# A four-layer graph network on one core: node stages load and store two groups of rows at a time

## The chip, the cores and the metric

The kernel runs on one core of one Trainium2 chip. The metric is device time in microseconds for one execution. Times before: 3703.67 us median of 3 runs, 3701.21 to 3707.44.

## What is computed

A table x of 50000 nodes by 128 numbers (fp32) and 25000 edges (src, dst, type), sorted by dst, go through four layers. Each layer normalises the rows of x, takes the positive part, applies a graph layer, and adds the result to x:

```python
h = jnp.maximum(_layernorm(x, axis=-1), 0.0)
x = x + _L0_gnn_ref(h, ...)   # per relation: sum over edges of h[src] @ w[type], + h @ loop + bias, relu
x = x + _L1_gnn_ref(h, ...)   # attention over edges, 4 heads, summed by src
x = x + _L2_gnn_ref(h, ...)   # two mean-aggregating layers, each with a layernorm
x = x + _L3_gnn_ref(h, ...)   # degree-normalised sum of h[src] @ W, and a self loop
```

## The kernel before, in words

There are five phases: REL (layer 0), ATT (layer 1), SAGE0 and SAGE1 (layer 2), GCN (layer 3). Each has an edge stage and then a node stage. The edge stage gathers rows by src with indirect transfers from POOL, multiplies them, sums them by destination within tiles of 128 edges, and scatters the sums to the table sums (attsums in ATT). In SAGE0, SAGE1 and GCN the sums of the edge stage are parked in SBUF and scattered in 49 rounds while the node stage already runs; load_s is then held until the rounds that it needs have landed (a value load of the due round, L648, and a wait).

**Node stage.** The 50000 rows are cut into 98 groups of 512 rows; in a group each partition holds K = 4 consecutive rows. A row has W = 132 numbers, 128 data and 4 columns for scales, 528 bytes; a group is 264 KB in 128 pieces of 2112 bytes. (In REL the input x, and in GCN the output, have 128 columns: 256 KB.) A ring of 16 slots, one group each, holds 8 slots for x, 4 for the sums and 4 for the output; in SAGE1 it is 4, 4 and 8.

All five engines run their own list of stages with lags (run_steps, L80 to 97): in turn t a stage with lag n works on group t-n. An engine does its list strictly in order, so a wait in one stage holds all that follow. The lists that matter:

- SP (L613 to 685) issues every transfer of the node stage: load_x, lag 0; load_s, lag 2 (ATT 0, SAGE1 3); load_x2, SAGE1 only, lag 5; store, lag 9 (ATT 6, SAGE1 10, GCN 7). In REL also row_stored (L675), lag 11, which tells POOL that rows are in memory. In REL load_s(g) waits until PE's products(g-4) are done, in GCN too, in SAGE0 for add_mean(g-4), in SAGE1 for mid_sd(g-4) on ACT, in ATT for weigh_heads(g-4). store(g) waits for row_ready(g).
- PE (L1286): products (L1321, L1324), lag 3, then the transposes turn_rows (L1299), lag 1, in REL and GCN; lags 2 and 0 in SAGE0 and SAGE1. The products go to 4 PSUM banks in turn in REL and SAGE1, 2 in SAGE0 and GCN.
- ACT in REL: roots of variances (L1044, L1095), take_turned (L1070), then normalise (L1056, n_h), lag 1.
- DVE in REL, in this order: statistics of x, lag 0; in_scales (L1715), lag 1; add_product (L1751), lag 4, which writes the output slot; out_scales (L1736); in_shifts (L1730), lag 1, after which ACT may normalise; out_shifts (L1743), lag 6, which gives row_ready; the statistics of the output, lag 5.
- DVE in ATT: denominators, out_scales (lag 3), inverses, statistics of the output (lag 2), out_shifts (L1743, lag 3, row_ready), weigh_heads (L1774, lag 0). POOL does add_x (L879), which writes the output slot. In GCN DVE's last stage, finish_gcn (L1836, lag 4), writes the output slot and gives row_ready. In SAGE0 mid_rows (L1799, lag 6) does so; add_mean (L1785) has lag 3.

What writes an output slot first waits in out_free (L516), until the store of the group that had the slot (four back, eight in SAGE1) has landed. The signals for transfers are semaphores of 8 slots each: loaded, loaded_s, loaded2, stored.

After REL's node stage POOL fetches destination rows for ATT (L855), in rounds held back by row_stored. Each phase begins when the stores of the one before have landed.

Of the kernel before, what the change touches and what calls it, by code (L numbers as in the profile page):

```python
# [5 lines left out]
class Step:  # L6
# [97 lines left out]
def gnn_stack_kernel(nc, x, src, dst, edge_type, w_rel, w_loop, b_loop, w_q, w_k, w_v,  # L104
# [9 lines left out]
    N, D = x.shape  # L114
# [25 lines left out]
    GROUPS = -(-N // GROUP)  # L140

    SLOTS = 8
    RING = 16
# [17 lines left out]
    with ctx:  # L161
# [213 lines left out]

        loaded = [Signal(sem(f"loaded{s}"), 16) for s in range(SLOTS)]
        loaded_s = [Signal(sem(f"loaded_s{s}"), 16) for s in range(SLOTS)]
        loaded2 = [Signal(sem(f"loaded2_{s}"), 16) for s in range(SLOTS)]
        stored = [Signal(sem(f"stored{s}"), 16) for s in range(SLOTS)]
# [78 lines left out]
        def stores_before(phase, s):  # L458

            return phase * (GROUPS // SLOTS + (1 if s < GROUPS % SLOTS else 0))  # L460

# [20 lines left out]
        def dense(slot):  # L482

            return ring_cells[:, slot * K * W:slot * K * W + K * D].rearrange("p (k d) -> p k d", k=K)
# [5 lines left out]
        def x_cols(phase, g, c):  # L490

            if phase == REL:
                at = g.mod(8) * K * W + K * D + (c - COL_A) * K
                return ring_cells[:, at:at + K]
            return x_rows(phase, g)[:, :, c]

        def x_col(phase, g, k, c):

            if phase == REL:
                at = g.mod(8) * K * W + K * D + (c - COL_A) * K + k  # L500
# [7 lines left out]
        def x_landed(eng, phase, g):  # L508
            s = g.mod(SLOTS)
            eng.wait_ge(loaded[s].sem, loaded[s].after(g.div(SLOTS), stores_before(phase, s)))  # L510

        def s_landed(eng, phase, g):
            s = g.mod(SLOTS)
            eng.wait_ge(loaded_s[s].sem, loaded_s[s].after(g.div(SLOTS), stores_before(phase, s)))

        def out_free(eng, phase, g):  # L516
# [36 lines left out]
        def _(sp):  # L553
# [35 lines left out]
            for phase in range(5):  # L589
# [11 lines left out]
                if phase > 0:  # L601
                    for s in range(SLOTS):
                        sp.wait_ge(stored[s].sem, 16 * stores_before(phase, s))

                def span(g):
                    if g.i is None and g.offset == GROUPS - 1:
                        return slice(N - GROUP, N)
                    return bass.ds(g.scaled(GROUP), GROUP)
# [4 lines left out]
                def load_x(g):  # L613
                    s = g.mod(SLOTS)
                    if phase == REL:

                        sp.wait_ge(n_y_used.sem, n_y_used.before(g, SLOTS, first(MATMUL, phase)))
                    elif phase == ATT:

                        sp.wait_ge(x_added.sem, x_added.before(g, SLOTS))  # L620
                    elif phase == SAGE0:

                        sp.wait_ge(n_turned.sem, n_turned.before(g, SLOTS, first(MATMUL, phase)))
                    elif phase == SAGE1:

                        sp.wait_ge(n_turned.sem, n_turned.before(g, 4, first(MATMUL, phase)))
                    else:

                        sp.wait_ge(row_ready.sem, row_ready.before(g, SLOTS, phase * GROUPS))
                    table = node_in[phase]  # L630
                    sp.dma_start(x_data(phase, g) if phase == REL else x_rows(phase, g), table[span(g), :].rearrange("(p k) c -> p k c", k=K))\
                        .then_inc(loaded[s].sem, 16)

                def load_s(g):
                    s = g.mod(SLOTS)
                    if phase == ATT:
                        sp.wait_ge(weighted_ready.sem, weighted_ready.before(g, S_SLOTS))
                    elif phase == SAGE0:
                        sp.wait_ge(n_y_used.sem, n_y_used.before(g, S_SLOTS, first(MATMUL, phase)))
                    elif phase == SAGE1:  # L640
                        sp.wait_ge(mid_sd_ready.sem, mid_sd_ready.before(g, S_SLOTS, first(MID_NORM, phase)))
                    else:
                        sp.wait_ge(n_y_ready.sem, n_y_ready.before(g, S_SLOTS, first(MATMUL, phase)))
# [1240 lines left out]
```

## Time and profile before

| | |
|---|---|
| median of 3 runs | 3703.67 us (3701.21 to 3707.44) |
| profiled execution | 3701.02 us, span 3699.3 us |
| busy in the span | PE 71%, PE weight load 62%, DVE 68%, ACT 53%, POOL 71% |
| granted TensorE clock | 0.895 of full speed |
| REL node stage | about 612 to 990 us |
| ATT node stage | about 1657 to 1920 us |
| SAGE0 node stage | about 2190 to 2502 us |
| SAGE1 node stage | about 2770 to 3125 us |
| GCN node stage | about 3400 to 3699 us |
| SP's and ACT's transfers | 241758 packets, 502.00 MB, 41.0% of 16 DMA engines |
| POOL's transfers | 90944 packets, 133.85 MB, 16.3% |

Busy time is that of instructions that compute; issuing a transfer is not counted. A stretch's DMA share is the mean busy share of 16 DMA engines. The idle time named before an instruction is put down to what came last by the profile.

### The profile page before, as it was taken

How to read it: one execution, taken by the hardware profiler on the slowest of the kernel's cores; microseconds unless marked ns; L12 is line 12 of the kernel's file. 1: busy time of each engine (PE TensorE's matmuls, PEld its weight loads, DVE VectorE, ACT ScalarE, POOL GpSimd, SP SyncE). 2: the span in 40 equal slices, each digit the busy share in tenths (PEclk: the TensorE clock that was granted, in tenths of full speed). 3: DMA queues.
4: the chain of work that ended last, by engine and by line, in shares of the span. 5: the costliest groups of instructions: out<-in, count | busy, mean ns of one | idle time of the engine just before them, and what ended most of it. 6: DMA issues, size and time to landing. Idle time of an engine off the chain costs nothing. (4 is left out here: it accounts for less than half of the span.)

```text
span 3699.3 us, 82926 instructions
## 1 busy us (share of the span) xinstructions
PE 2617.9 (71%) x19724; PEld 2288.0 (62%) x19724; DVE 2511.4 (68%) x11513; ACT 1948.6 (53%) x5393; POOL 2612.2 (71%) x2673
## 2 busy tenths in 40 slices
PE   3899998888466666630018887767888775887888
PEld 3899997666465555530007765546776665776777
DVE  5677776889555445538864448883448887665998
ACT  1333334777454444421117777763446664776777
POOL 3677773666788888855457778767778784777876
PEclk9999999999787777765559999998999998999999
DMA  7544444888433333339972239982229997222998
GB/s 277 215 149 140 147 147 136 268 267 269 125 42 41 41 41 41 41 50 317 311 229 53 52 109 297 294 287 67 52 60 332 335 337 246 53 52 79 309 311 287
DMA packets 336597, 638.73 MB, mean 173 GB/s; under 512 B 62000, under 2 KB 90832, under 8 KB 335208
## 3 DMA queue, kind: packets, MB, share of 16 engines
q1 hardware_dynamic: 241758, 502.00, 41.0%
q0 software_dynamic: 90944, 133.85, 16.3%
q10 hardware_dynamic: 3786, 1.65, 0.2%
q8 instruction: 41, 0.67, 0.1%
q14 instruction: 68, 0.56, 0.0%
HBM read 371.35 MB, written 277.50 MB: 175 GB/s over the span
## 5 line engine op out<-in xcount | busy, mean ns | idle before, releaser
L750 POOL DMA_INDIRECT got<-rows,gidx x588 | 606.3, 1031 | 225.8 <-issue 173.3
L797 POOL DMA_INDIRECT sums<-got,sidx x588 | 614.9, 1046 | 168.7 <-issue 156.5
L1056 ACT ACTIVATE n_h<-ring 128x128 f32<-128x128 f32 x1176 | 482.7, 482 | 56.5 <-DVE ring L1730 45.8
L971 ACT ACTIVATE psum_out<-bank 128x132 f32<-128x132 f32 x784 | 218.8, 279 | 531.4 <-PE bank L1223 530.7
L1324 PE MATMUL bank<-ring,ident 128*128 128x128 f32 x2352 | 459.3, 277 | 0.0
L1204 PE MATMUL bank<-parked 128*128 128x128 f32 x3136 | 388.7, 278 | 11.9 <-DVE parked L1558 11.9
L1189 PE MATMUL bank<-ident,e_h 128*128 128x128 f32 x588 | 96.0, 287 | 408.0 <-ACT e_h L934 408.0
L1204 PEld LDWEIGHTS bank<-parked 128*128 128x128 f32 x3136 | 371.5, 194 | 13.7 <-issue 8.6
L811 POOL DMA_INDIRECT attsums<-ring,sidx x196 | 312.3, 1594 | 80.2 <-issue 64.5
L1324 PEld LDWEIGHTS bank<-ring,ident 128*128 128x128 f32 x2352 | 361.6, 194 | 0.0
L1461 DVE COPY gidx<-src_i 128x4 int32 (+1 forms) x227 | 45.2, 199 | 465.2 <-DMA got<-rows,gidx 204.4
L1223 PE MATMUL bank<-psum_out,eq 128*128 128x132 f32 x1568 | 351.7, 306 | 12.2 <-ACT psum_out L971 9.7
L1219 PE MATMUL bank<-msg,eq 128*128 128x132 f32 x1568 | 322.5, 287 | 24.5 <-issue 17.8
L1299 PE MATMUL bank<-ident,n_h 128*128 128x128 f32 x1176 | 200.1, 295 | 194.3 <-ACT n_h L1056 191.1
L1321 PE MATMUL bank<-w_t,n_ht 128*128 128x128 f32 x1568 | 284.6, 296 | 64.0 <-DMA ring<-sums 63.7
L1189 PEld LDWEIGHTS bank<-ident,e_h 128*128 128x128 f32 x588 | 65.5, 143 | 427.5 <-ACT e_h L934 409.7
L934 ACT ACTIVATE e_h<-got 128x128 f32<-128x128 f32 x588 | 282.5, 484 | 41.7 <-DMA got<-rows,gidx 34.2
L855 POOL DMA_INDIRECT got<-rows,didx x196 | 197.0, 1005 | 143.4 <-SPq L678 76.6
L1321 PEld LDWEIGHTS bank<-w_t,n_ht 128*128 128x128 f32 x1568 | 221.9, 198 | 117.0 <-DMA ring<-sums 90.9
L1299 PEld LDWEIGHTS bank<-ident,n_h 128*128 128x128 f32 x1176 | 129.2, 145 | 248.4 <-ACT n_h L1056 248.1
L1223 PEld LDWEIGHTS bank<-psum_out,eq 128*128 128x128 f32 x1568 | 236.1, 190 | 67.5 <-ACT psum_out L971 25.3
L1558 DVE SCALAR_TENSOR_TENSOR parked<-bank,e_ht 128x256 f32<-128x256 f32 x784 | 267.9, 417 | 9.4 <-PE bank L1159 7.8
(183 smaller groups left out, 7250.7 us busy)
## 6 DMA issues: line engine op xcount, KB each, us to landing
ring<-sums SPq DMA_DIRECT2D x392, 264.0 KB
ring<-rows SPq DMA_DIRECT2D x392, 264.0 KB, 4.7
rows<-ring SPq DMA_DIRECT2D x294, 264.0 KB
attsums<-parked SPq DMA_DIRECT2D x49, 528.0 KB
rows<-parked SPq DMA_DIRECT2D x49, 528.0 KB
ring<-attsums SPq DMA_DIRECT2D x98, 264.0 KB
rowsg<-ring SPq DMA_DIRECT2D x98, 264.0 KB
ring<-rowsg SPq DMA_DIRECT2D x98, 264.0 KB
```

Of the source, the lines that this page charges most:

```text
L750: pool.indirect_dma_start(out=got[:, b, j, 0:width], out_offset=None, in_=table[:, :], in_offset=bass.IndirectOffsetOnAxis(ap=gidx[:, b, j ...
L797: pool.indirect_dma_start(out=sums[:, :], out_offset=bass.IndirectOffsetOnAxis(ap=sidx[:, b, j:j + 1], axis=0), in_=got[:, b, j, :], in_of ...
L811: pool.indirect_dma_start(out=attsums[:, :], out_offset=bass.IndirectOffsetOnAxis(ap=sidx[:, b, j:j + 1], axis=0), in_=att_out[:, b, j, :] ...
L934: last = nc.scalar.activation(e_h[:, b, j, :], got[:, c, j, 0:D], ACT.Relu, bias=got[:, c, j, COL_C:COL_C + 1], scale=got[:, c, j, COL_A:C ...
L1056: last = nc.scalar.activation(n_h[:, b, k, :], x_data(phase, g)[:, k, :], ACT.Relu, bias=x_col(phase, g, k, COL_C), scale=x_col(phase, g, ...
L1204: last = nc.tensor.matmul(o, lhsT=e_htm[:, h, rel, at:at + P], rhs=w_rel_sb[:, rel, :], start=(rel == 0), stop=(rel == NREL - 1))
L1219: nc.tensor.matmul(o, lhsT=eq[:, b, j, 0, :], rhs=msg[:, b, j, :], start=True, stop=False)
L1223: nc.tensor.matmul(o, lhsT=eq[:, b, j, 1, :], rhs=carried, start=False, stop=True)\
L1299: last = nc.tensor.transpose(bank[b][:, k * P:(k + 1) * P], rows, ident[:, :])
L1321: last = nc.tensor.matmul(o, lhsT=n_ht[:, b, k * P:(k + 1) * P], rhs=node_w[phase], start=(bias is None), stop=(not summed and k == K - 1))
L1324: last = nc.tensor.matmul(o, lhsT=ident[:, :], rhs=s_rows(phase, g)[:, k, 0:D], start=False, stop=(bias is None or k == K - 1))
L1558: last = nc.vector.scalar_tensor_tensor(out=e_htm[:, h, rel, :], in0=type_bank[b][:, at:at + 2 * P], scalar=float(rel), in1=e_ht[:, b, at: ...
```

## The change

Groups are loaded and stored by pairs. A pair is 1024 rows, and each partition holds eight consecutive rows of it: four in the even group's slot, four in the odd one's. Every transfer of a node stage moves 528 KB in 128 pieces of 4224 bytes (512 KB in 4096 where a row has 128 columns). An odd group's load and an even group's store do nothing; a load waits for what its later group (g+1) needs, a store for the odd group's row. The number of slots, the lags and the work by group on the engines stay. The semaphores count by pair, four of each kind. The last pair is the last 1024 rows, which overlap the pair before. row_stored adds 2 for each pair.

```diff
+    def pair(self):
+        return self.back(self.offset % 2).div(2)
...
+    PAIR = 2 * GROUP
+    PAIRS = GROUPS // 2
...
+    PSLOTS = SLOTS // 2
...
         def out_free(eng, phase, g):
             back = OUT_SLOTS.get(phase, 4)
             if g.i is None and g.offset < back:
                 return
-            o = g.back(back)
-            s = o.mod(SLOTS)
-            eng.wait_ge(stored[s].sem, stored[s].after(o.div(SLOTS), stores_before(phase, s)))
+            o = g.back(back).pair()
+            s = o.mod(PSLOTS)
+            eng.wait_ge(stored[s].sem, stored[s].after(o.div(PSLOTS), stores_before(phase, s)))
...
                 def load_x(g):
-                    s = g.mod(SLOTS)
+                    if g.offset % 2:
+                        return
+                    s = g.pair().mod(PSLOTS)
+                    later = g.back(-1)
                     if phase == REL:
-                        sp.wait_ge(n_y_used.sem, n_y_used.before(g, SLOTS, first(MATMUL, phase)))
+                        sp.wait_ge(n_y_used.sem, n_y_used.before(later, SLOTS, first(MATMUL, phase)))
...
                     table = node_in[phase]
-                    sp.dma_start(x_data(phase, g) if phase == REL else x_rows(phase, g), table[span(g), :].rearrange("(p k) c -> p k c", k=K))\
+                    sp.dma_start(slot_pair(g.mod(X_SLOTS.get(phase, 8)), table.shape[1]), rows_of(table, g))\
                         .then_inc(loaded[s].sem, 16)
...
                 def load_s(g):
-                    s = g.mod(SLOTS)
+                    if g.offset % 2:
+                        return
+                    s = g.pair().mod(PSLOTS)
+                    later = g.back(-1)
...
-                        sp.wait_ge(n_y_ready.sem, n_y_ready.before(g, S_SLOTS, first(MATMUL, phase)))
+                        sp.wait_ge(n_y_ready.sem, n_y_ready.before(later, S_SLOTS, first(MATMUL, phase)))
...
-                        due = sp.value_load(due_i[0:1, CHASED.index(phase), at(g)], min_val=base, max_val=base + ROUNDS)
+                        due = sp.value_load(due_i[0:1, CHASED.index(phase), at(later)], min_val=base, max_val=base + ROUNDS)
...
                 def store(g):
-                    s = g.mod(SLOTS)
+                    if g.offset % 2 == 0:
+                        return
+                    s = g.pair().mod(PSLOTS)
                     sp.wait_ge(row_ready.sem, row_ready.after(g, phase * GROUPS))
...
                     table = node_out[phase]
-                    sp.dma_start(table[span(g), :].rearrange("(p k) c -> p k c", k=K),
-                                 out_data(phase, g) if phase == GCN else out_rows(phase, g)).then_inc(stored[s].sem, 16)
+                    slots = OUT_SLOTS.get(phase, 4)
+                    sp.dma_start(rows_of(table, g), slot_pair(RING - slots + g.back(1).mod(slots), table.shape[1]))\
+                        .then_inc(stored[s].sem, 16)
```

slot_pair gives two neighbouring slots as one run of cells in each partition, rows_of the table's 1024 rows as eight to a partition. Where rows have 128 columns, the data of the two groups now stand side by side in the pair of slots, with the scale columns behind them (dense, dense_col).

## Rows read from the trace of the kernel before

**Rows 1.** Stretches REL to GCN: us, busy PE, PEld, DVE, ACT, POOL, PEclk, DMA, GB/s

```profile
627.00:961.00 334.00, 287.94 (x2034) 232.21 (x2031) 298.84 (x1990) 249.18 (x665) 213.26 (x267) 0.99 0.86 260
1662.00:1914.00 252.00, 0.00 (x0) 0.00 (x0) 222.36 (x1254) 28.55 (x96) 124.95 (x98) 0.50 0.93 308
2217.00:2497.00 280.00, 196.49 (x1167) 141.48 (x1166) 230.91 (x1019) 209.32 (x537) 212.33 (x256) 0.94 0.91 293
2777.00:3119.00 342.00, 270.37 (x2007) 226.59 (x2007) 306.18 (x1253) 212.23 (x680) 254.76 (x275) 0.98 0.97 329
3414.00:3697.00 283.00, 239.37 (x1938) 218.82 (x1937) 255.63 (x1421) 221.83 (x570) 210.21 (x270) 1.00 0.94 301
```

**Rows 2.** Waits in REL's node stage: us in total, times, longest

```profile
DVE ring L1751 <- DMA rows<-ring: 27.7, 40, 1.5
...
SPq L650 <- PE bank L1324: 171.6, 93, 9.6
```

**Rows 3.** Timeline of REL's node stage: start us, us, engine, line, operation

```profile
796.25 0.38 SPq L671 DMA_DIRECT2D rows<-ring  x1
...
796.50 0.17 DVE L1743 SCALAR_TENSOR_TENSOR ring<-out_mv,ring 128x4 f32<-128x4 f32 x1
...
799.71 0.35 SPq L671 DMA_DIRECT2D rows<-ring  x1
799.78 0.69 DVE L1751 SCALAR_TENSOR_TENSOR ring<-bank,ring 128x512 f32<-128x512 f32 x1 [0.71 <-DMA rows<-ring]
...
800.48 0.13 DVE L1730 SCALAR_TENSOR_TENSOR ring<-in_mv,ring 128x4 f32<-128x4 f32 x1
...
800.69 1.65 ACT L1056 ACTIVATE n_h<-ring 128x128 f32<-128x128 f32 x4 [0.67 <-DVE ring L1730]
...
802.78 0.16 DVE L1715 RECIPROCAL ring<-in_sd 128x4 f32<-128x4 f32 x1
...
803.81 0.69 DVE L1751 SCALAR_TENSOR_TENSOR ring<-bank,ring 128x512 f32<-128x512 f32 x1 [0.87 <-DMA rows<-ring]
...
804.97 0.39 PE L1324 MATMUL bank<-ring,ident 128*128 128x128 f32 x2
...
806.11 0.35 SPq L671 DMA_DIRECT2D rows<-ring  x1
```

**Rows 4.** Waits in ATT's node stage

```profile
POOL ring L879 <- DMA rows<-ring: 96.1, 64, 2.3
```

**Rows 5.** Timeline of ATT's node stage

```profile
1675.32 0.34 SPq L671 DMA_DIRECT2D rows<-ring  x1
...
1678.46 1.26 POOL L879 TENSOR_TENSOR ring<-n_t,ring 128x512 f32<-128x512 f32 x1 [1.10 <-DMA rows<-ring]
...
1785.95 1.26 POOL L879 TENSOR_TENSOR ring<-n_t,ring 128x512 f32<-128x512 f32 x1 [2.14 <-DMA rows<-ring]
1786.08 1.15 DVE L1743 SCALAR_TENSOR_TENSOR ring<-out_mv,ring 128x4 f32<-128x4 f32 x1
```

**Rows 6.** Timeline of SAGE1's node stage

```profile
2903.17 0.31 ACT L1078 ACTIVATE mid_sd<-mid_mv,eps_col 128x4 f32<-128x4 f32 x1
...
2904.68 0.33 SPq L650 DMA_DIRECT2D ring<-sums  x1
...
2909.17 0.49 PE L1321 MATMUL bank<-w_t,n_ht 128*128 128x128 f32 x2 [0.38 <-DMA ring<-sums]
```

**Rows 7.** Timeline of GCN's node stage

```profile
3523.65 1.13 DVE L1836 SCALAR_TENSOR_TENSOR ring<-bank,ring 128x128 f32<-128x128 f32 x4
...
3530.23 0.35 SPq L671 DMA_DIRECT2D out_dram<-ring  x1
```

**Rows 8.** SP's DMA queue, 150 to 550 us and 1700 to 1900 us: packets, MB, share

```profile
q1 hardware_dynamic: 10656, 40.01, 26.5%
...
q1 hardware_dynamic: 33228, 62.40, 95.1%
```

**Rows 9.** A stretch of ATT's edge stage, columns as in rows 1

```profile
1200.00:1250.00 50.00, 28.73 (x183) 26.38 (x183) 25.68 (x105) 22.41 (x66) 40.84 (x31) 0.77 0.33 40
```

More of the change, by code:

```diff
@@ L374, in gnn_stack_kernel @@
                     a_h, a_turned, a_ht, a_qkv, a_q, a_logit, a_exp, a_res, a_sum, a_out, a_eq]
[L376 to L379, printed above, removed]
+        loaded = [Signal(sem(f"loaded{s}"), 16) for s in range(PSLOTS)]
+        loaded_s = [Signal(sem(f"loaded_s{s}"), 16) for s in range(PSLOTS)]
+        loaded2 = [Signal(sem(f"loaded2_{s}"), 16) for s in range(PSLOTS)]
+        stored = [Signal(sem(f"stored{s}"), 16) for s in range(PSLOTS)]
         in_var = Signal(sem("in_var"), 1)
@@ L492, in x_cols @@
             if phase == REL:
[L493 removed]
+                at = dense_col(g.mod(8), c)
                 return ring_cells[:, at:at + K]
@@ L508, in x_landed @@
         def x_landed(eng, phase, g):
[L509 to L510 removed]
+            p = g.pair()
+            s = p.mod(PSLOTS)
+            eng.wait_ge(loaded[s].sem, loaded[s].after(p.div(PSLOTS), stores_before(phase, s)))
         def s_landed(eng, phase, g):
[L513 to L514 removed]
+            p = g.pair()
+            s = p.mod(PSLOTS)
+            eng.wait_ge(loaded_s[s].sem, loaded_s[s].after(p.div(PSLOTS), stores_before(phase, s)))
         def out_free(eng, phase, g):
@@ L601, in _, with rows_of @@
                 if phase > 0:
-                    for s in range(SLOTS):
+                    for s in range(PSLOTS):
                         sp.wait_ge(stored[s].sem, 16 * stores_before(phase, s))
[L605 to L608, printed above, removed]
+                def rows_of(table, g):
+                    p = g.pair()
+                    if p.i is None and p.offset == PAIRS - 1:
+                        at = slice(N - PAIR, N)
+                    else:
+                        at = bass.ds(p.scaled(PAIR), PAIR)
+                    return table[at, :].rearrange("(p k) c -> p (k c)", k=2 * K)
                 def at(g):
@@ L677, in row_stored @@
-                    sp.wait_ge(stored[s].sem, stored[s].after(g.div(SLOTS), stores_before(phase, s)))
-                    sp.sem_inc(rows_stored.sem, 1)
+                    if g.offset % 2 == 0:
+                        return
+                    p = g.pair()
+                    s = p.mod(PSLOTS)
+                    sp.wait_ge(stored[s].sem, stored[s].after(p.div(PSLOTS), stores_before(phase, s)))
+                    sp.sem_inc(rows_stored.sem, 2)
                 s_lag = {REL: 2, ATT: 0, SAGE0: 2, SAGE1: 3, GCN: 2}[phase]
@@ L685, in _ @@
                 run_steps(sp, stages, GROUPS, SLOTS, behind=SLOTS)
-            for s in range(SLOTS):
+            for s in range(PSLOTS):
                 sp.wait_ge(stored[s].sem, 16 * stores_before(5, s))
@@ L728, in _ @@
                 if phase > 0:
-                    for s in range(SLOTS):
+                    for s in range(PSLOTS):
                         pool.wait_ge(stored[s].sem, 16 * stores_before(phase, s))
@@ L1813, in shift_x2 @@
                 def shift_x2(g):
-                    s = g.mod(SLOTS)
+                    p = g.pair()
+                    s = p.mod(PSLOTS)
                     rows = out_rows(phase, g)
-                    dve.wait_ge(loaded2[s].sem, loaded2[s].after(g.div(SLOTS)))
+                    dve.wait_ge(loaded2[s].sem, loaded2[s].after(p.div(PSLOTS)))
                     nc.vector.reciprocal(rows[:, :, COL_DIS], root_deg[:, g.mod(DEEP), :])
```

41 lines of the change are left out of this document (22 added, 19 removed).

## The prediction

> **What bounds the kernel now.** Only the five node stages change, so I read their stretches first [rows 1]; in each the reader should hold DVE's busy time and the DMA share against the length. REL: DVE 298.84 of 334 us, DMA 0.86. ATT: 222.36 of 252, 0.93. SAGE0: 230.91 of 280, 0.91. SAGE1: 306.18 of 342, 0.97. GCN: 255.63 of 283, 0.94. No engine is full, so I looked next for who waits for whom. In REL, SP waits 171.6 us at load_s for PE, and DVE's add (L1751) waits 40 times for "rows<-ring", a store that has not landed [rows 2]. In ATT, POOL's add (L879) waits for such a store in 64 of 98 groups, 96.1 us in all [rows 4]. So the output slots are on the path in both. There are four of them there, and the change leaves four.
>
> The order of time in REL shows a ring of waits [rows 3]. Call the add at 799.78 group G. It waited for store(G-4), issued at 796.25. store(G-3) left at 799.71, though L1743 had made its rows ready at 796.67: it stood behind load_s(G+4) in SP's queue, which waits until products(G) end. By PE's order products(m) come after the transposes of m+1. So store(g) needs products(g+3), these the transposes of g+4, these n_h(g+4), and that in_shifts(g+4) (L1730), which DVE does in the turn of add(g+1), just after it. Then add(g+4) needs the store. The ring spans three groups. Its parts [rows 3]: add to L1730 0.70; L1730 to the end of n_h 1.86 (800.48 to 802.34); to the end of the products 3.02 (805.36); to the store's issue 0.75 (806.11); from a store's issue to the add that it frees 3.53 (796.25 to 799.78) or 4.10 (799.71 to 803.81). That is 9.9 to 10.4 us, so 3.3 to 3.5 a group, and the stage runs at 334/97 = 3.44 [rows 1]. On this agreement I build.
>
> **REL after.** A store is issued for an odd g only, with (g-1, g), and load_s ahead of it now waits for the products of g+4, the later group of its pair, not g+3. It frees the add of g+3, the next even group. So the ring runs from add(G+1), odd, to add(G+2), even: one group instead of three; one DVE turn, add(G) to add(G+1), closes the pair. For a pair: the turn 3.2 (799.78 to L1715's end, 802.94); 0.70 + 1.86 + 3.02 + 0.75 = 6.33; then the store [rows 3]. Its 3.53 to 4.10 were for 264 KB behind a load of 264 KB in the same queue, and both double. ATT's stretch moved 62.40 MB in 200 us at a share of 95.1% [rows 8]: 328 GB/s, 0.82 us for 264 KB. Two more make 4.9 to 5.7; I take 5.1, near the lower row, since the queue will be emptier. Sum 14.6 us. PE is then busy less than half of the time, and its clock will not stay at 0.99 [rows 1]. In ATT's edge stage, with PE busy 28.73 of 50 us, 0.77 was granted [rows 9]; 3.02/0.77 is 0.9 more; I add 0.8 (nothing to 3.0, which is the half level throughout). A pair takes **15.4 us** against 6.89. The first two pairs find free slots, so 47 x 8.5 = **+400**. Bounds 14.0 and 17.0: +335 to +475.
>
> The Trainium skill (DMA: Bandwidth & Descriptors, Anatomy of one DMA) fits a transfer as 2.0 us plus its bytes over 436 GB/s, from the GpSimd path: 3.2 us for 528 KB. The trace has 3.53 already for 264 KB behind a load, which is more. By that figure, called an estimate, a pair would be 1.9 us shorter and REL +310.
>
> **ATT after.** add_x(G), G even, needs the store of (G-4, G-3), issued once L1743 has done G-3. Ring for a pair: add_x(G), 1.26; stats(G), then L1743(G-1), which makes the next pair whole. L1743 does not finish while POOL adds: the one at 1786.08 took 1.15 us and ended at 1787.23, POOL's add ran from 1785.95 to 1787.21 [rows 5]. add_x(G+1) will follow add_x(G) at once, as one store frees both, so L1743 ends after two adds, 2.8 us with their starts; 0.2 to the issue; then the store. The nearest row is a 264 KB store early in the stage, 1675.32 to 1678.46, 3.14 [rows 5]; 0.8 more makes 3.9 (3.5 to 4.8). The pair takes **6.9 us** against 2 x 252/97 = 5.2: 47 x 1.7 = **+80** (+55 to +120).
>
> **SAGE0 after.** The row is finished two turns after the add_mean for which load_s waits. The ring covers four groups: from what load_s waits for to its issue 1.2 (measured in SAGE1 [rows 6]), 0.6 to the store, 5.1 for it, two turns of DVE work, 2 x 230.91/98 = 4.7: 11.6, or 2.9 a group, where the stage has 280/98 = 2.9 now [rows 1]. At the edge, not over it; the last pair moves a little later: **+5** (0 to +25).
>
> **SAGE1 after.** Eight output slots; stores do not bind. load_s(G) waits for mid_sd(G-3), one group later than now, and PE waits for its data already: 1.2 from mid_sd's end (2903.48) to the issue (2904.68), 4.5 on to the first product (2909.17), which waited for it [rows 6]. Twice the size adds 0.8 to 1.4 us a pair, of which half may show: up to +30. For the change: SP's issues halve; and the pieces of 4224 B in the zeroing took 26.5% of 400 us for 40.01 MB, 42 ns a KB on one DMA engine, those of 2112 B in ATT 49 [rows 8], while DMA stands at 0.97. The floor is DVE, 306.18/98 = 3.1 a group against 3.5: -35. I take **0** (-35 to +30).
>
> **GCN after.** store(g), g odd, stands behind load_s(g+5), which waits for products(g+2), and these need the bank that finish_gcn(g) frees. The store frees finish_gcn(g+3). From a finish's end, 3524.78, to the store issued after the products two groups on, 3530.23: 5.45 [rows 7]; store 5.1; finish 1.13; a turn 255.63/98 = 2.6. That is 14.3 for four groups, 3.57 each, against 283/97 = 2.92 [rows 1]: 94 x 0.65 = **+60** (+20 to +85).
>
> What costs nothing: 784 transfers fewer for SP to issue, behind the waits above (in SAGE1 it counts, above); the end's waits on four semaphores instead of eight; loads of x, issued two turns or more ahead where they need some 5 us. If those turns shrank the loads would be next.
>
> **Sum.** 400 + 80 + 5 + 0 + 60 = +545. The profiled execution took 3701.02 us (span 3699.3), 2.65 under the median of 3703.67. 3701 + 545 is **4246 us**.
>
> **The rivals.** (a) *Stores leave when their rows are ready; load_s does not hold them.* REL's pair is then 3.2, 1.0 to L1743's end, 0.2, and a store of 4.6, 9.0 in all: +100; GCN loses its ring: with ATT +185, to +235 if some of GCN stays, 3910 us. Against it: 799.71 against 796.67 [rows 3], and SP's 171.6 us for PE [rows 2]. Chance 0.10. (b) *Faster.* The slots are free in time, and issue and transfer decide. Its place is SAGE1, DMA at 0.97, -35, and ATT, 0.93, down towards DVE's 222.36/98 = 2.27 a group, at most -30 and rather -15: 3650 us. It decides only where a 528 KB store lands inside the slack of the slots, and REL has none: 40 waits with single groups. The Trainium skill (DMA: Bandwidth & Descriptors, Rules for kernel authors) says to coalesce many small transfers into one large; by that rule this is the outcome. Chance 0.03. (c) *Nothing seen*: the pairs still go in 2112-byte pieces and the waits are covered. The zeroing moved 74 transfers of 528 KB in 10656 packets [rows 8], 74 x (128 + 16), so such pieces stay whole; and neither ring depends on them. Chance 0.02. (d) *Worse*: PE at the half level through REL and GCN and stores of 5.7 us: +475, +85, +120, 4380 us and up. Chance 0.08.
>
> **How the numbers follow.** The forecast has 0.77; its own range, REL's bounds and the others' not all added, is 4100 to 4390. Misreadings of my own rings, and half of (d), carry it to 4400; to leave no more than 0.2 outside, I reach down towards (a): **3990 to 4400**. A measurement can tell 0.2%, 7 us, from no change. Slower 0.95, same 0.02, faster 0.03.
>
> **What would show it.** L1751 starting in unequal steps, one of about 3 us and one of about 12, with 47 waits for "rows<-ring" of 7 to 9 us; SP's load_s in REL still released by PE, and the store 0.6 us after it; PE's clock in REL under 0.9; L879 in twos, 6.9 us apart; in GCN, DVE waiting for "out_dram<-ring" in every second pair; SAGE0 and SAGE1 within 35 us of now. I am wrong if REL's pair takes under 12 us, for then SP or PE is less tied than I read; or if SAGE1 moves by more than 35 us.

## The result, and the profile after

The changed kernel takes 4281.79 us (median of 4 runs, 4279.14 to 4283.87) where the kernel before takes 3705.56 (4 runs beside them): a ratio of 1.156, 95% interval 1.155 to 1.158, or 576 us more. The profiled execution took 4283.87 us, its span 4282.2. The forecast was 545 more.

I read the profile after in the same order as before, first the node stages. The columns are us from and to, length, then busy PE, PEld, DVE, ACT and POOL with their counts, granted clock, DMA share, GB/s; the rows are REL, ATT, SAGE0, SAGE1, GCN.

```profile
631.00:1420.00 789.00, 397.25 (x2036) 329.11 (x2035) 311.36 (x1993) 246.45 (x666) 212.79 (x267) 0.71 0.37 110
2123.00:2409.00 286.00, 0.00 (x0) 0.00 (x0) 223.66 (x1261) 28.84 (x97) 122.16 (x98) 0.50 0.81 269
2696.00:3005.00 309.00, 215.47 (x1239) 155.78 (x1237) 238.90 (x1080) 222.44 (x569) 224.78 (x270) 0.91 0.84 277
3299.00:3651.00 352.00, 275.05 (x1924) 233.81 (x1923) 302.29 (x1230) 208.37 (x657) 236.68 (x260) 0.92 0.92 309
3942.00:4279.00 337.00, 248.83 (x1938) 220.21 (x1937) 254.25 (x1421) 226.87 (x570) 210.65 (x270) 1.00 0.80 251
```

Against [rows 1]: DVE does the same work in REL, 311 us of it, but now in 789 us instead of 334. Every other stage grows too, none shrinks, and DMA's share falls in all five. As a share of its stretch no engine is clearly busier than before, so the time went into waits. Only PE is busy for longer in REL, 397 us instead of 288 for the same work, at a granted clock of 0.71 instead of 0.99. From the first to the last write of an output slot (DVE's add L1751, now L1782, POOL's L879, now L910, and so on), in us:

| stage | before | after | more | forecast |
|---|---|---|---|---|
| REL | 334.1 | 788.0 | 453.9 | 400 (335 to 475) |
| ATT | 250.6 | 283.5 | 32.9 | 80 (55 to 120) |
| SAGE0 | 289.4 | 302.2 | 12.8 | 5 (0 to 25) |
| SAGE1 | 332.1 | 351.1 | 19.0 | 0 (-35 to 30) |
| GCN | 281.8 | 336.3 | 54.5 | 60 (20 to 85) |

That is 573 of the 583 us by which the span grew. The waits in REL's stage, in us in total, times, longest; L675 is load_s, L699 the store, L709 row_stored:

```profile
POOL got L886 <- SPq L709: 549.6, 45, 67.8
DVE ring L1782 <- DMA rows<-ring: 469.2, 46, 11.1
...
SPq L675 <- PE bank L1355: 331.6, 47, 17.1
```

DVE waited 27.7 us for stores before, in 40 waits of at most 1.5 [rows 2]. Now 46 of the 49 pairs wait some 10.2 us each, and SP stands at load_s for PE 47 times, 331.6 us in all. POOL's fetches for the next stage wait longer still, but they wait for the same stores, and the first gather of ATT comes 31 us after REL's last add, as it did before with 30.

Two turns of REL in order of time. The reader should follow one ring, from the add at 1009.37, of an even group, to the next one that had to wait, at 1026.84:

```profile
1009.37 0.69 DVE L1782 SCALAR_TENSOR_TENSOR ring<-bank,ring 128x512 f32<-128x512 f32 x1 [10.54 <-DMA rows<-ring]
...
1012.30 1.11 PE L1330 MATMUL bank<-ident,n_h 128*128 128x128 f32 x4 [8.78 <-ACT n_h L1087]
...
1012.72 0.66 DVE L1782 SCALAR_TENSOR_TENSOR ring<-bank,ring 128x512 f32<-128x512 f32 x1
...
1013.38 0.13 DVE L1761 SCALAR_TENSOR_TENSOR ring<-in_mv,ring 128x4 f32<-128x4 f32 x1
...
1013.88 0.80 PE L1352 MATMUL bank<-w_loop_sb,n_ht 128*128 128x128 f32 x2
...
1013.95 1.64 ACT L1087 ACTIVATE n_h<-ring 128x128 f32<-128x128 f32 x4
...
1017.45 1.06 PE L1330 MATMUL bank<-ident,n_h 128*128 128x128 f32 x4
...
1020.43 0.39 PE L1355 MATMUL bank<-ring,ident 128*128 128x128 f32 x2
...
1020.98 0.33 SPq L675 DMA_DIRECT2D ring<-sums  x1
1021.51 0.35 SPq L699 DMA_DIRECT2D rows<-ring  x1
...
1026.84 0.69 DVE L1782 SCALAR_TENSOR_TENSOR ring<-bank,ring 128x512 f32<-128x512 f32 x1 [10.86 <-DMA rows<-ring]
```

The odd group's add follows 3.35 us after the even one's. Its turn gives L1761, and ACT has the rows normalised at 1015.59. PE cannot turn them yet: it is still at the products of the group before, which run from 1013.35 to 1017.45. Then transposes and products to 1020.82, load_s at 1020.98, the store behind it at 1021.51, and 5.33 us later the slot is free. The steps of DVE's adds go 3.3 and 13.9 us by turns here, about 17.2 us for a pair; their medians over the stage are 3.4 and 13.7. The last wait, for the store, takes 5.16 us from issue to the freed add in the median of the 46 pairs.

ATT, the same way:

```profile
2205.51 2.51 POOL L910 TENSOR_TENSOR ring<-n_t,ring 128x512 f32<-128x512 f32 x2 [3.16 <-DVE n_t L1805]
...
2207.63 0.42 DVE L1774 SCALAR_TENSOR_TENSOR ring<-out_mv,ring 128x4 f32<-128x4 f32 x1
...
2208.24 0.36 SPq L699 DMA_DIRECT2D rows<-ring  x1
...
2211.36 2.49 POOL L910 TENSOR_TENSOR ring<-n_t,ring 128x512 f32<-128x512 f32 x2 [3.33 <-DMA rows<-ring]
```

POOL's adds go in twos, 5.85 us apart (2205.51 to 2211.36), and the store of 528 KB takes 3.12 us from its issue to the add that it frees (median over the stage 3.16). The load just ahead of it in SP's queue was issued 2.88 us before it (load_s at 2205.36); in REL that was 0.53 us.

In the three other stages, the waits that were not there or were short before (a wait in SAGE0, two of SP's in SAGE1, one in GCN; L684 is load_x2):

```profile
DVE ring L1830 <- DMA rowsg<-ring: 56.1, 37, 4.2
...
SPq L425 <- ACT mid_sd L1109: 87.3, 45, 3.6
SPq L684 <- DMA rows<-ring: 71.5, 39, 5.3
...
DVE ring L1868 <- DMA out_dram<-ring: 56.7, 39, 2.7
```

And SP's queue over the whole execution, packets, MB and share of 16 engines:

```profile
q1 hardware_dynamic: 128862, 501.95, 35.3%
```

Before it was 241758 packets, 502.00 MB and 41.0%. So the pieces did double. But 35.3% of 4282 us is 1512 us and 41.0% of 3699 is 1517: over the whole execution the larger pieces took the DMA engines the same time for the same bytes. In ATT's stage alone it is the same: 269 GB/s at a share of 0.81 against 308 at 0.93 [rows 1], 332 and 331 for a full share.

### The profile page after: what moved, and what is told of

The parts are those of the page before. It is cut to its first block and busy times, and to the rows that moved or that the text cites. A ratio compares the mean times of both kernels' runs of the same rounds, so it can differ in the third digit from the quotient of the medians.

```text
span 4282.2 us, 79914 instructions
## 1 busy us (share of the span) xinstructions
PE 2765.4 (65%) x19724; PEld 2414.6 (56%) x19724; DVE 2517.0 (59%) x11513; ACT 1955.1 (46%) x5393; POOL 2604.2 (61%) x2673
## 3 DMA queue, kind: packets, MB, share of 16 engines
q1 hardware_dynamic: 128862, 501.95, 35.3%
## 5 line engine op out<-in xcount | busy, mean ns | idle before, releaser
L1330 PE MATMUL bank<-ident,n_h 128*128 128x128 f32 x1176 | 235.2, 334 | 578.6 <-ACT n_h L1087 578.0
L1330 PEld LDWEIGHTS bank<-ident,n_h 128*128 128x128 f32 x1176 | 162.1, 170 | 624.1 <-ACT n_h L1087 623.8
L1355 PE MATMUL bank<-ring,ident 128*128 128x128 f32 x2352 | 511.7, 304 | 0.0
L1355 PEld LDWEIGHTS bank<-ring,ident 128*128 128x128 f32 x2352 | 413.4, 220 | 0.0
L1782 DVE SCALAR_TENSOR_TENSOR ring<-bank,ring 128x512 f32<-128x512 f32 x98 | 66.0, 673 | 473.3 <-DMA rows<-ring 469.2
L1352 PE MATMUL bank<-w_t,n_ht 128*128 128x128 f32 x1568 | 299.7, 307 | 68.7 <-DMA ring<-sums 68.5
L1352 PEld LDWEIGHTS bank<-w_t,n_ht 128*128 128x128 f32 x1568 | 235.2, 209 | 120.9 <-DMA ring<-sums 80.1
L1101 ACT ACTIVATE n_ht<-bank 128x512 f32<-128x512 f32 x294 | 175.1, 596 | 251.7 <-PE bank L1330 249.2
```

The lines of the kernel that those rows point to most:

```text
L1330: last = nc.tensor.transpose(bank[b][:, k * P:(k + 1) * P], rows, ident[:, :])
L1352: last = nc.tensor.matmul(o, lhsT=n_ht[:, b, k * P:(k + 1) * P], rhs=node_w[phase], start=(bias is None), stop=(not summed and k == K - 1))
L1355: last = nc.tensor.matmul(o, lhsT=ident[:, :], rhs=s_rows(phase, g)[:, k, 0:D], start=False, stop=(bias is None or k == K - 1))
```

## The experiments

All are edits of the changed kernel unless said otherwise. They ran in three lots, each on one chip. On the third the kernel before takes 3703 us, as on the first result's chip; on the other two, called the slower chips here, 4571 and 4575. There, in every stage that uses TensorE, ACT and DVE had waits of up to 12.7 us that the trace gives to no instruction, at lines that read PE's results, while PE's own rows end long before; the cause was not looked for. ATT's node stage, which uses no PE, was as long in fill_x2, where it is as the change has it, as on the first chip (281.9 and 283.5 us). The kernel before has no profile on a slower chip. So the slower chips serve for the steps of REL's ring and for ATT; totals are compared within a chip.

**Which part of the ring costs.** Four edits, each meant to open one link.

*The store first in SP's list:*

```diff
-stages = [(load_x, 0), (load_s, s_lag), (load_x2, 5), (store, store_lag)]
+stages = [(store, store_lag), (load_x, 0), (load_s, s_lag), (load_x2, 5)]
```

> The changed kernel with one thing altered: in SP's list of the node stages the store stands first, ahead of load_x and load_s, in all five stages. Ring theory (a pair's store stands behind load_s, which waits for products four groups on): the store leaves when its rows are ready, so REL's pair falls from 16.7 us to the turn 3.35 + 1.0 to the end of L1774's row + 0.2 + store 5.1 = 9.7 us, the adds' span from 788 to about 470 us; GCN's adds' span from 336 to about 285; ATT up to 30 us less, SAGE0 10 less; in all about 3870 us. Slots theory (four output slots with stores by pairs are too few, whatever SP's order): no change, 4282 within 15 us. Size theory (a 528 KB transfer lands late by itself): no change beyond 60 us, since every transfer is still there.

*Stores by group, loads by pairs* (one semaphore a group for the stores; the rows of a group are four of the eight of each partition):

```diff
-                    if g.offset % 2 == 0:
-                        return
...
-                    sp.dma_start(rows_of(table, g), slot_pair(RING - slots + g.back(1).mod(slots), table.shape[1]))\
+                    sp.dma_start(half_of(node_out[phase], g),
+                                 out_data(phase, g) if phase == GCN else out_rows(phase, g)).then_inc(stored[s].sem, 16)
```

> The changed kernel with loads by pairs as they are, but each group's four rows of a partition stored by themselves as soon as they are ready (264 KB in pieces of 2112 bytes, one semaphore a group). Ring theory: the store of an odd group still stands behind load_s and frees the add four groups on, two groups after the in_shifts that started the ring: 0.64 + 1.86 + products 3.0 to 5.0 + 0.75 + store 3.5 to 4.1 = 10 to 12.5 for a pair, about 11: REL's adds 788 to about 540 us, ATT back to 250 (33 less), GCN 20 less, in all about 3980 us. Size theory: each pair only gains what its store is shorter, 1.0 to 1.6 us, 50 to 80 us in REL, in all about 4190. If the pairs of the loads cost nothing: about 3710.

*Loads by group, stores by pairs:*

```diff
-                    if g.offset % 2:
-                        return
...
-                    later = g.back(-1)
+                    later = g
...
-                    sp.dma_start(slot_pair(g.mod(X_SLOTS.get(phase, 8)), table.shape[1]), rows_of(table, g))\
+                    sp.dma_start(x_data(phase, g) if phase == REL else x_rows(phase, g), half_of(table, g))\
```

> The changed kernel with stores by pairs as they are, but loads by group as before (264 KB in pieces of 2112 bytes, load_s waiting for what its own group needs; in the chased stages an even group waits for the round of its pair, since its rows reach over the pair). SP also counts a semaphore after each wait, some 0.05 us each, not on the path. Ring theory: load_s ahead of the store waits for products three groups on instead of four, so the ring is 0.64 + 1.86 + products 3.0 to 5.0 + 0.75 + store 5.1 = 11.4 to 13.4 for a pair without the turn of 3.35, about 12.5: REL's adds 788 to about 610 us, in all about 4090 us. Slots theory (pairs of stores in four slots are the whole cost): no change, about 4280. Size theory: loads of half the size land 0.8 to 1.4 us earlier, but they are not waited for in REL: about 4270.

*Eight output slots in REL and ATT:*

```diff
-        OUT_SLOTS = {SAGE1: 8}
+        OUT_SLOTS = {REL: 8, ATT: 8, SAGE1: 8}
...
+            if phase == ATT:
+                cells, at = got[:, :, :, :].rearrange("p b j c -> p (b j c)"), o - 4
+            elif o < 6:
+                cells, at = psum_out[:, :, :, :].rearrange("p b j c -> p (b j c)"), o - 4
+            else:
+                cells, at = eq[:, :, :, :, :].rearrange("p b j h c -> p (b j h c)"), o - 6
+            return cells[:, at * K * W:(at + n) * K * W]
```

> The changed kernel with eight output slots instead of four in REL and ATT; the four more lie in buffers of the edge stages that are idle then. Lists, sizes and waits stay. Ring theory: a store now frees the add eight groups back, so the ring is four groups longer and no longer binds; REL goes at DVE's pace, 3.05 to 3.4 us a group, adds' span 300 to 335 us instead of 788 and PE's clock back over 0.9; ATT 250 or less instead of 283; in all about 3790 us. Size theory (pairs of 528 KB are late for their readers or crowd the DMA engines): REL's adds stay above 400 us, in all above 3900.

These four ran on a slower chip (before: 4571 us). They took 4596, 4803, 4806 and 4527 us, ratios 1.003 (0.999 to 1.006), 1.051 (1.042 to 1.059), 1.052 (1.045 to 1.059) and 0.989 (0.985 to 0.992). The changed kernel with only an idle filler in REL (fill_x2, below) took 1.096 (1.088 to 1.103) on such a chip and stands for it. DVE's adds in REL (shortest, median and longest in ns, first and last start in us) and what ended the waits before them. First the kernel with the store first in the list:

```profile
L1782 DVE SCALAR_TENSOR_TENSOR ring<-bank,ring x98: 655/691/693, 740.6 to 1138.8; 128x512 f32<-128x512 f32 x98
...
  DMA rows<-ring: 42.9, 19
  PE bank L1355: 38.6, 22
```

With single stores:

```profile
L1791 DVE SCALAR_TENSOR_TENSOR ring<-bank,ring x98: 650/691/693, 746.6 to 1349.2; 128x512 f32<-128x512 f32 x98
...
  DMA rows<-ring: 293.4, 46
```

With single loads:

```profile
L1793 DVE SCALAR_TENSOR_TENSOR ring<-bank,ring x98: 654/679/693, 746.3 to 1316.1; 128x512 f32<-128x512 f32 x98
...
  DMA rows<-ring: 264.1, 46
```

And in fill_x2, whose REL stage is the change's but for idle matmuls:

```profile
L1786 DVE SCALAR_TENSOR_TENSOR ring<-bank,ring x98: 648/691/693, 742.4 to 1560.1; 128x512 f32<-128x512 f32 x98
...
  DMA rows<-ring: 459.2, 44
```

The steps are medians over the stage.

| | REL's adds, us | a pair's two steps, us | forecast for the pair |
|---|---|---|---|
| pairs (fill_x2) | 818 | 3.3 + 13.8 | |
| store first | 398 | 3.1 + 5.1 | 9.7 |
| single stores | 603 | 3.1 + 9.9 | 11 |
| single loads | 570 | 3.1 + 9.2 | 12.5 |
| eight slots | 361 | 3.1 + 4.6 | 6.1 to 6.8 |

SP's order alone gives back 420 of 818 us, with every transfer, size and slot as in the change; so it was not slots alone, nor size alone. Making either the loads or the stores single gives back 215 to 248, with 46 waits for stores still there; against the 361 us of eight slots that is about half of what the pairs cost on this chip, so about half is left either way. The order between these two was not as expected: 603 us with single stores where 540 were forecast, 570 with single loads where 610 were. With four more slots no wait for a store is left before the add; what remains is 59 us of waits, 17 for PE and 43 that the trace gives to no instruction.

Why single loads did better shows in the time from a store's issue to the add that it frees. With single loads:

```profile
1013.46 0.36 SPq L710 DMA_DIRECT2D rows<-ring  x1
...
1017.29 0.69 DVE L1793 SCALAR_TENSOR_TENSOR ring<-bank,ring 128x512 f32<-128x512 f32 x1 [5.47 <-DMA rows<-ring]
```

That is 3.83 us, in the median of the stage 3.7, for a store of 528 KB some 0.7 us behind a load of 264 KB. Behind a load of 528 KB the same store took 5.2 us (fill_x2), and a store of 264 KB 4.5 (single stores). So of the 4.7 us by which single loads shorten a pair, some 1.5 come from the size of the load just ahead and not from what that load waits for. With the store first it took 4.2 us, the last load being 1.9 us ahead. Size, then, is a part of the cost, through what stands ahead of the store in the queue.

GCN agrees, as far as a stage with PE can be read there: its last line took 470.4 us with the store first, 472.9 with single stores, 476.5 with single loads, and 503 to 505 in slots8 and fill_x2, which leave GCN as the change has it.

ATT answered differently. Its adds took 281.8, 284.1 and 281.4 us with the store first, single stores and single loads, as in the changed kernel (283.5), and 239.0 with eight slots. SP's order is nothing there, and one half of the pairs costs as much as both: in ATT the even group's single store falls into the turn of the loads, 0.6 us behind a load_s of 528 KB, and then takes 5.2 us (median of 44) to the add that it frees, where the pair's store, 3.0 us behind that load, takes 3.2. One such turn, L687 being load_s and L708 the store (its row holds two issues, of which the one at 2146.29 frees the add):

```profile
2145.68 0.35 SPq L687 DMA_DIRECT2D ring<-attsums  x1
...
2146.29 2.60 SPq L708 DMA_DIRECT2D rows<-ring  x2
...
2152.31 2.48 POOL L919 TENSOR_TENSOR ring<-n_t,ring 128x512 f32<-128x512 f32 x2 [3.97 <-DMA rows<-ring]
```

I had expected single stores to give the 33 us back; they gave none.

**The same, and pairs against single groups with free slots.** The first of these is the kernel with the store first again, the second has both edits, eight slots and the store first, and the last one makes both in the kernel before:

```diff
+OUT_SLOTS = {REL: 8, ATT: 8, SAGE1: 8}
+stages = [(store, store_lag), (load_x, 0), (load_s, s_lag), (load_x2, 5)]
```

> The same kernel as store_first, again, since the chip of its first run took 4571 us for the kernel before instead of 3705, with TensorE slower in every stage. There REL's adds went in pairs of 8.5 us (3.1 + 5.4) in 398 us. Where the kernel before takes 3705: ring theory as before, pair 8 to 9.7 us, adds' span 390 to 470, GCN's 285 to 300, in all about 3830 to 3870 us. Slots or size theory: 4220 to 4282.

> The changed kernel with eight output slots in REL and ATT and the store first in SP's list. Every wait for a slot that was read in REL, ATT and GCN is gone. If only the rings cost: REL 300 to 335 us, ATT 240 to 250, GCN 285, SAGE0 and SAGE1 as before: 3650 to 3720 us where the kernel before takes 3705. If a load or store of 528 KB costs by itself (it lands later, its readers wait): above 3750.

> The kernel before (single groups) with the same two alterations, eight output slots in REL and ATT and the store first. With the pairs of slots8_first beside it this tells what pairs are worth when no slot binds. Ring theory: REL's adds from 334 to 305 to 315 us (DVE is busy 3.05 us a group), ATT's from 251 to 240, GCN's from 282 to 275: 3640 to 3670 us where the kernel before takes 3705. If fewer and larger transfers are worth anything in themselves, slots8_first is faster than this one by 0.2% or more; I expect it 0 to 1% slower. If REL before was not held by the ring: 3705.

This chip was a slower one too (before: 4575 us), so the totals expected where the kernel before takes 3705 were not put to the test. Ratios: 1.004 (1.000 to 1.009), 0.979 (0.973 to 0.986) and 1.005 (1.000 to 1.009). REL's adds with the store first took 391.6 us: the 398 nearly repeats. With free slots the pairs took 370.7 us in REL and 239.7 in ATT, the single groups 385.4 and 247.4 (the profiled execution of the pairs took 4565 us, 1.5% over their median). I had expected the pairs 0 to 1% behind; they are 2.5% ahead. That rests on few executions, and little can be built on it: on this chip single stages with PE differ by more between the two profiles (SAGE1 392 and 420 us, SAGE0 390 and 382). ATT's node stage has no PE in it and can be trusted here, single groups first, pairs second:

```profile
1836.00:2084.00 248.00, 0.00 (x0) 0.00 (x0) 218.59 (x1252) 28.55 (x96) 123.39 (x98) 0.50 0.94 313
```

```profile
1827.00:2067.00 240.00, 0.00 (x0) 0.00 (x0) 211.85 (x1248) 28.53 (x96) 123.04 (x98) 0.50 0.91 319
```

The share of DMA is smaller and the stage 8 us shorter, 3%. There is one such profile of single groups; three of pairs with eight slots gave 235.5 to 239.7 us. The difference sits at the line of DVE that first reads the loaded sums (den): it waited 6.7 us in all for loads and took 31.1 us with single groups, 1.6 and 24.6 with pairs. So larger transfers are worth something in this stage, where DMA stood at 0.94, once no slot binds. Whether it is the pieces or the number of transfers was not tried.

**TensorE's clock, and load_x2.** Two alterations in stages that don't touch each other:

```diff
+                    if phase == REL and g.offset % 2:
+                        for _ in range(28):
+                            nc.tensor.matmul(bank[7][:, :], lhsT=ones_bf[:, :],
+                                             rhs=bias_bf[:, 0, :, :].rearrange("p k d -> p (k d)"), start=True, stop=True)
...
-stages = [(load_x, 0), (load_s, s_lag), (load_x2, 5), (store, store_lag)]
+stages = [(load_x, 0), (load_s, s_lag), (load_x2, 6), (store, store_lag)]
```

> The changed kernel with two alterations in different stages. REL: after the products of each odd group PE does 28 more matmuls of 512 columns into a bank that nobody reads, in the 8.8 us in which it would idle. SAGE1: load_x2 has lag 6 instead of 5 in SP's list, so that it waits for a store issued three turns before it, not two. Clock theory (my ring is right and only PE's part was mis-sized: after 8.8 us idle PE runs at the half level for about 6 us, the products of the even group take 4.2 us instead of 2.4 and hold the transposes of the next): the idle spell is gone, PE stays at the full level, and REL's pair falls from 17.2 (3.3 + 13.9) to 3.3 + 0.7 + 1.86 + 3.0 + 0.75 + 5.1 = 14.7 to 15.2 us, the adds' span from 788 to about 710 us. If PE's clock is not on the ring: no change in REL, 788 within 10. SAGE1, block theory (SP stands at load_x2 71 us in all and is late with load_s and load_x): its adds' span 351 falls to 335 and SP's wait at load_x2 to under 10 us; otherwise 351 stays. In all about 4190 us where the kernel before takes 3705.

In REL the steps stayed 3.3 and 13.8 us, and the clock at 0.70: it fell in the middle of the filler, and the even group's products ran at the half level as before. SAGE1's adds took 370.5 us, where the changed kernel with lag 5, in the six runs of its edits on slower chips, took 383 to 399. A second filler, of six matmuls of 128 rows by 512 fp32 columns:

```diff
+                        for _ in range(6):
+                            nc.tensor.matmul(bank[7][:, :], lhsT=ident[:, :],
+                                             rhs=w_t[:, :, :].rearrange("p n d -> p (n d)"), start=True, stop=True)
```

> The changed kernel with another filler than in fill_x2, whose 28 matmuls with 3 rows did not hold the clock (it fell to the half level in the middle of them): after the products of each odd group of REL, PE does six matmuls of 128 rows by 512 fp32 columns into a bank nobody reads, some 5 us of the 8.8 us of idling. Clock theory: PE stays at the full level, the even group's products take 2.4 instead of 4.2 us, and REL's pair falls from 17.2 to 14.7 to 15.2 us (adds' span about 720 us). If the pair stays at 17 with PE's clock near 1.0, PE's level is not on the ring. If the clock stays at 0.7, nothing is told.

It ran once, on the third chip: 4279 us, REL's adds 799 (787 without it). The clock stood at 1.00 during the filler. PE's timeline:

```profile
1008.52 5.32 PE L1360 MATMUL bank<-w_t,ident 128*128 128x512 f32 x12
1017.47 1.12 PE L1330 MATMUL bank<-ident,n_h 128*128 128x128 f32 x4 [3.64 <-ACT n_h L1087]
...
1019.05 0.80 PE L1352 MATMUL bank<-w_loop_sb,n_ht 128*128 128x128 f32 x2
```

The filler left 3.64 us idle before the transposes, and they still took 1.12 us, the half level's duration. So neither filler tells whether a full clock would shorten the ring; that stays open.

**The references, and a version by stage.** The two kernels as they are, and the changed kernel with what had helped so far:

> The changed kernel as it is. The chips of the experiments so far took 4571 and 4575 us for the kernel before, where the first took 3706, so the experiments need it as their own reference. Ring theory: its ring in REL hardly uses what is slow there, so REL's adds go in 3.3 + 13.9 = 17.2 us and 790 to 830 us as on the first chip, and the whole is about 5000 to 5050 us (fill_x2, which has the same REL stage but for idle matmuls, took 5020), a ratio of 1.09 to 1.11 to the kernel before. If the slower chip costs the change as much as the kernel before in every stage, the ratio stays at 1.156, 5290 us.

> The kernel before as it is, for its profile on the chips of the experiments. REL's adds 334 us on the first chip; here by PE 370 to 400 us, ATT's 250 to 255, the other stages longer by what PE loses. The waits for slots in REL (40 of them, 1.6 us each on the first chip) are partly taken over by waits for PE.

```diff
+OUT_SLOTS = {REL: 8, ATT: 8, SAGE1: 8}
+stages = [(load_x, 0), (load_s, s_lag), (load_x2, 6)]
+stages.insert(3 if phase == SAGE1 else 0, (store, store_lag))
```

> The changed kernel with what the runs so far gave, stage by stage: eight output slots in REL and ATT, the store first in SP's list in all stages but SAGE1, and load_x2 with lag 6. slots8 and slots8_first took 0.989 and 0.979 of the kernel before. SAGE1's adds were 391 to 394 us with load_x2 at lag 5 or the store first, 370 with lag 6 (fill_x2): 20 us less. In all 0.970 to 0.985 of the kernel before; if SAGE1's 20 us were the chip's spread, 0.985 to 1.0.

This was the third chip. The changed kernel took 4273 us, a ratio of 1.155 (1.153 to 1.157), so 5000 us was wrong for this chip and the first result repeats: REL 787.4, ATT 282.4, SAGE0 301.3, SAGE1 346.5, GCN 335.5 us. The kernel before took 3703 us (3704 in its profiled execution), with 336.8, 252.5, 285.0, 330.3 and 282.3; the 1.6 us for each of its waits in the expectation above should be 0.7, 27.7 us in 40 [rows 2]. The version by stage took 3716 us, 1.004 (1.003 to 1.005) of the kernel before, not 0.970 to 0.985: against the changed kernel 557 us are gone. Its stages, from REL to GCN:

```profile
631.00:942.00 311.00, 286.24 (x2036) 230.07 (x2034) 305.40 (x1993) 250.54 (x666) 204.78 (x257) 1.00 0.85 277
1655.00:1892.00 237.00, 0.00 (x0) 0.00 (x0) 209.27 (x1255) 28.54 (x96) 124.04 (x98) 0.50 0.92 323
2180.00:2484.00 304.00, 209.42 (x1239) 151.06 (x1237) 236.73 (x1076) 222.14 (x569) 226.95 (x270) 0.93 0.84 281
2778.00:3119.00 341.00, 271.29 (x1929) 230.02 (x1927) 301.02 (x1230) 207.51 (x657) 236.61 (x259) 0.93 0.91 319
3411.00:3704.00 293.00, 238.35 (x1933) 217.82 (x1931) 257.19 (x1418) 224.48 (x570) 209.78 (x270) 1.00 0.90 289
```

REL is at DVE's limit now, 305 of 311 us, with pairs of 528 KB and the clock at 1.00; ATT is 15 us shorter than before the change. Both beat the kernel before on this chip, by 27 us (309.9 against 336.8) and 17 (235.5 against 252.5). Of these 44 us, 12 are lost between the two stages: with REL shorter, POOL has 24 of its 196 fetches for ATT left at REL's last add, not 16, and the first gather of ATT's edge stage comes 42 us after that add, not 30. SAGE0, SAGE1 and GCN give back the rest: 297.7, 340.2 and 292.1 against 285.0, 330.3 and 282.3, 32 us in all. In GCN the store now leaves in time, and 44 of the 54.5 us come back; in SAGE1 SP's wait at load_x2 is gone, but SP now waits 129 us at load_x for PE's transposes, 42 us in the changed kernel, and 340.2 us is hardly under the 341.3 to 351.1 of three profiles with lag 5 on such chips. What is left in SAGE0 and GCN reads, in that order, as loads that come late:

```profile
DVE n_t L1834 <- DMA ring<-sums: 54.9, 36, 3.5
...
DVE in_stats L1723 <- DMA ring<-rows: 13.6, 29, 0.8
```

Pairs in REL and ATT alone, with eight slots and single groups elsewhere, would be some 30 us under the kernel before by these rows, 44 less 12; at ATT's last add this profile stood 29 us ahead. That is an estimate; it wasn't run.

## Why the prediction was right, point by point

**REL, forecast +400, measured +454.** The mechanism is the one forecast. Each link was opened by a run: the store behind load_s (the pair fell from 17.1 to 8.2 us), the pair's loads with their later group's condition, and the pair's store (12.3 and 12.9), the four slots (7.7). Term by term, from the timeline above:

| term of the pair | forecast | measured |
|---|---|---|
| the turn, even add to odd add | 3.2 | 3.35 |
| to L1761 | 0.70 | 0.66 |
| to the end of n_h | 1.86 | 2.21 |
| PE still at the products before | 0 | 1.86 |
| transposes and products | 3.02 + 0.8 | 3.37 |
| to the store's issue | 0.75 | 0.69 |
| the store to the add it frees | 5.1 | 5.33 |
| sum | 15.4 | 17.5 |

The term that was mis-sized is the clock's. I took 0.8 us as a stretch of the products of the group in the ring. They ran at the full level in the end; it is the group before whose products ran at the half level (four of L1352's pairs at 0.63 to 0.80 us instead of 0.39 to 0.49), 4.1 us instead of 2.4, and they stand ahead of the ring's transposes in PE's order. The cost is a queue's, not a stretch's. That this is what the 1.86 us would vanish with is argued from the rows, since both fillers failed.

**The store.** 5.1 was forecast and 5.33 measured in the pair above, 5.16 in the median, behind a load of 528 KB issued some 0.5 us ahead in the same queue. The working had a slip that didn't matter: 3.53 and two more times 0.82 make 5.2, not 4.9. That both the store and the load ahead of it count by their size was the right idea; halving the load took 1.5 us off, halving the store 0.7, where 0.8 had been taken for each. The Trainium skill (DMA: Bandwidth & Descriptors, Anatomy of one DMA) gives 3.2 us for this size, an estimate by its fit for the GpSimd path. ATT's store, with the nearest load issued 2.9 us before it, took 3.12: page and row agree there, and differ where another transfer of the size is just ahead.

**ATT, +80 forecast, +33 measured, below the range.** The ring was right and two of its terms were too long: the store 3.12 instead of 3.9, and L1774 ended 2.54 us after the first add's start instead of 2.8. That makes 5.85 instead of 6.9 us, and 47 x (5.85 - 5.2) = 31. I had added 0.8 us for twice the bytes to a row of 3.14 for 264 KB; it did not come. That row had a load 1.5 us ahead of the store, the pair's store has it 2.9 us ahead, and over the stage the single stores before had taken 3.8 to 3.9 us in the median. The store was quicker farther behind the load; the engines were also less full (0.81 against 0.93), and the two were not parted.

**GCN, +60 and +54.5.** Right, and with the store first 44 of it came back, so it was the store behind load_s, as said.

**SAGE0, +5 and +13.** "At the edge, not over it" was a little over it: 37 waits for rowsg<-ring, 56.1 us in all, mostly taken out of slack.

**SAGE1, 0 and +19.** The saving that I had taken from longer pieces (42 against 49 ns a KB) isn't there: in ATT's stage pieces of 4224 B took the same engine time for a byte as those of 2112 B. The step that failed is "eight output slots; stores do not bind". They do not bind DVE, but load_x2 takes a slot too, and SP does it in the load of an even group, two turns after the store it needs; before, it was three. SP stood there 39 times, 71.5 us, with load_x and load_s behind it. With lag 6 the wait was gone, and the stage was 13 us or more shorter on a slower chip than in runs with lag 5, and 1 to 11 us on the third and first chips, where the profiles of the changed kernel differ by 5 themselves; how much of the 19 it explains stays open.

**The rivals.** (a), stores that leave when their rows are ready, was false of this kernel and true of the edit with the store first: there the pair took 8.2 us where 9.0 had been worked out. (b) was false as a whole, and its rule (the Trainium skill, DMA: Bandwidth & Descriptors, Rules for kernel authors: put many small transfers together) held only where the slots were free, by 3% in ATT. (c) fell with the packets, nearly halved. (d)'s clock was half true: 0.71 over REL, but GCN kept 1.00.

## What to carry to other kernels

Before making transfers larger, count the slots in units of the new size: four slots with pairs are two, and the ring from a store to the write it frees loses a whole round. Then read what stands ahead of the store in the queue of the engine that issues it: a load's wait for its later group held the stores in REL and GCN, and moving the store ahead of it gave back 420 of REL's 818 us without touching a byte. The size of that load counts too: just behind 528 KB the store took 1.5 us longer than behind 264. When a stage starts to wait, see whether TensorE comes back at its half level, as it did in REL and not in GCN, and look for whose work stands behind its slow products. And a stage that gets shorter can leave work of another engine over for the next one, as POOL's fetches here.

## What the runs showed of the hardware

- After 8.78 us idle, PE's matmuls ran at 1.2 GHz for some 6 us (granted clock 0.50 from 1012.3 to 1018.4, then 1.00; four of 0.63 to 0.80 us for two, then 0.39 from 1018.45), and 45 of REL's 49 pairs have such an idle stretch, of 8 to 9 us. Five microseconds of fp32 matmuls in that gap, leaving 3.64 us idle, did not prevent it, nor did 28 matmuls of 3 rows by 512 columns back to back, during which the level fell.
- Two chips took 4571 and 4575 us for the kernel before where two others took 3706 and 3703. ATT's node stage, without TensorE, was the same length (281.9 us in fill_x2, 283.5 in the changed kernel on the first chip); in the others ACT and DVE waited up to 12.7 us at lines that read PE's results, with no cause in the trace. Similar edits gave 0.979 to 0.989 of the kernel before there and 1.004 (in the version by stage) on the third chip.
- From its issue to the instruction that it frees, a store of 528 KB took 3.2 us (median, ATT) with the last load issued 3.0 us before it, 3.7 with a load of 264 KB 0.7 us ahead, and 5.2 with one of 528 KB 0.6 us ahead (both in REL). A store of 264 KB took 5.2 in ATT 0.6 us behind a load of 528 KB, longer than the 528 KB store there.
- Pieces of 4224 bytes took the DMA engines as long for a byte as pieces of 2112.
